# Weight preparation moved into the attention layer; power weights and message products as split halves on Trainium2

## The reference, cut to what matters

```python
# layer 0: masked attention
A = exp(tanh(x @ q @ (x @ k).T / sqrt(D) / 8) * 8) * adj; A = A / A.sum(-1)
x = layernorm(x + A @ x @ v)
# layer 1: gated, 5 steps, m_in = m_out = adj @ h
u3 = h @ u3_w.T + u3_b
z = sigmoid(av @ w3_w.T + w3_b + u3);  r = sigmoid(av @ w4_w.T + w4_b + u3)
hv = tanh(av @ w5_w.T + w5_b + (r * h @ u5_w.T + u5_b));  h = (1 - z) * h + z * hv
# layer 2: powers 0 to 3 of the adjacency, each with weights of its own
y = sum_k adj^k @ x @ weight_k        # both adjacencies are adj: weights 1..3 are summed in pairs
x = layernorm(x + y)
# layer 3: messages
f = relu(x @ psi_w + psi_b); m = (adj * adj).T @ f
h = relu(concat(m, x) @ phi1_w + phi1_b); x = layernorm(x + h @ phi2_w + phi2_b)
```

## Time and profile before

| | |
|---|---|
| median of 3 runs | 1480.62 us (1480.22, 1480.62, 2062.51) |
| profiled execution | 1478.63 us, span 1476.8 us |
| TensorE busy | 1405.0 us (95%) |
| TensorE weight load busy | 1223.4 us (83%) |
| VectorE busy | 1048.6 us (71%) |
| ScalarE busy | 930.1 us (63%) |
| GpSimd busy | 671.1 us (45%) |
| mean granted TensorE clock | 0.981 |

### The profile page before, as it was taken

The page is one execution under the profiler, slowest core; times in us unless marked ns, Lnnn a source line. Parts: engine busy times, 40 slices in busy tenths (PEclk is TensorE's granted clock), DMA queues, the critical chain, the costliest instruction groups (busy, mean ns, idle before and its releaser), DMA issues. The chain is left out here.

```text
span 1476.8 us, 27170 instructions
## 1 busy us (share of the span) xinstructions
PE 1405.0 (95%) x8813; PEld 1223.4 (83%) x8813; DVE 1048.6 (71%) x2558; ACT 930.1 (63%) x1666; POOL 671.1 (45%) x628
## 2 busy tenths in 40 slices
PE   3999996999999999999999999997699999999995
PEld 3888885888888888888888888886699999999993
DVE  2788884777777777777777777776466666666663
ACT  1666663677776777767777677775356566556653
POOL 0111113666687666786666866667222222211122
PEclk9999997999999999999999999999799999999998
DMA  2111111000000000010000100000001111111101
GB/s 75 37 43 43 43 35 57 1 0 0 0 34 25 1 0 0 19 38 0 0 0 4 53 0 0 0 0 14 30 22 44 44 43 43 43 43 43 36 25 32
DMA packets 46063, 35.76 MB, mean 24 GB/s; under 512 B 3140, under 2 KB 37704, under 8 KB 46024
## 3 DMA queue, kind: packets, MB, share of 16 engines
q1 hardware_dynamic: 46024, 35.27, 7.4%
HBM read 10.10 MB, written 8.39 MB: 13 GB/s over the span
## 5 line engine op out<-in xcount | busy, mean ns | idle before, releaser
L540 POOL TENSOR_TENSOR rh_lo<-rh,rh_hi 128x512 fp32r<-128x512 f32 x160 | 207.0, 1294 | 229.4 <-ACT rh_hi L661 219.7
L820 POOL TENSOR_TENSOR c_rstd<-c_var_eps,c_minus_half 128x12 f32<-128x12 f32 x37 | 84.0, 2270 | 347.3 <-DVE c_var_eps L1048 347.3
L546 POOL TENSOR_TENSOR h_lo<-h,h_hi 128x512 fp32r<-128x512 f32 x160 | 208.1, 1301 | 12.8
L675 DVE TENSOR_TENSOR psum<-psum,h 128x512 f32<-128x512 f32 x160 | 111.9, 700 | 105.1 <-ACT psum L665 105.1
L661 ACT CAST rh_hi<-rh 128x512 fp32r<-128x512 f32 x160 | 99.9, 624 | 121.2 <-DVE rh L693 121.2
L594 PE MATMUL psum<-adj_t_hi,hn_hi 128*128 128x256 f32 x640 | 172.6, 303 | 0.6 <-DVE m_lo L687 0.6
L658 ACT ACTIVATE psum<-psum,bias_cols 128x512 f32<-128x512 f32 x160 | 106.0, 662 | 105.8 <-PE psum L612 105.8
L693 DVE TENSOR_TENSOR rh<-psum,h 128x512 f32<-128x512 f32 x160 | 110.7, 692 | 70.8 <-ACT psum L658 70.7
L596 PE MATMUL psum<-adj_t_hi,hn_lo 128*128 128x256 f32 x640 | 159.4, 283 | 0.0
L832 PE MATMUL psum<-wcat,x2t 128*128 128x128 f32 x1024 | 137.2, 277 | 0.7 <-ACT x2t L984 0.7
L832 PEld LDWEIGHTS psum<-wcat,x2t 128*128 128x128 f32 x1024 | 126.5, 194 | 1.6 <-ACT x2t L984 1.1
(11 more groups left out here) (161 smaller groups left out, 3875.3 us busy)
## 6 DMA issues: line engine op xcount, KB each, us to landing
x_in<-in_x_dram SPq DMA_DIRECT2D x32, 256.0 KB, 2.8
h<-state SPq DMA_DIRECT2D x32, 256.0 KB, 2.3
y1t<-state SPq DMA_DIRECT2D x32, 256.0 KB, 2.4
out_dram<-res SPq DMA_DIRECT2D x32, 256.0 KB, 2.3
conv_in<-in_L_gnn_weight_dram SPq DMA_DIRECT2D x1, 448.0 KB, 3.3
w_in<-in_L_gnn_w_w_dram SPq DMA_DIRECT2D x3, 128.0 KB, 2.3
adj_n<-in_adj_dram SPq DMA_DIRECT2D x1, 256.0 KB, 2.7
u_in<-in_L_gnn_u_w_dram SPq DMA_DIRECT2D x2, 64.0 KB, 2.3
```

Of the source, the lines that this page charges most:

```text
L540: pool.tensor_tensor(rh_lo[:, q, :], rh[:, q, :], rh_hi[:, q, :].bitcast(F32), ALU.subtract).then_inc(rh_lo_done, 1)
L546: pool.tensor_tensor(h_lo[:, q, :], h[:, (g - 1) % G, :], h_hi[:, q, :].bitcast(F32), ALU.subtract).then_inc(h_lo_done, 1)
L675: dve.tensor_tensor(cb, cb, hg, ALU.subtract).then_inc(dif_done, 1)
```

## The change

`setup` as a stage goes; its work stands in `attention_layer`. SyncE issues the first input tile first, then the adjacency, then between the input tiles the gate weights (slot 1) and the rest (slot 3). ScalarE's queue issues q, k and v. TensorE transposes q, k and the adjacency ahead of slot 0 and the gate weights after slot 1. GpSimd sums the gate weights and the power weights, and splits the power weights `wcat` (in reversed order of powers) into `wc_hi`, `wc_lo` and `phi1m` into `phi1m_hi`, `phi1m_lo`. The gate weights lie in joint tiles (`wg_hi`, `ug_hi`), with the same products in the gated layer.

In `graph_conv_layers` x2 transposed is split (`x2t_hi` by ScalarE, `x2t_lo` by VectorE), and `weights(q, pair, c)` makes three fp32r products of 256 columns for each batch: two powers at once. PSUM banks 0 and 1 hold powers 3 and 2, banks 2 and 3 powers 1 and 0, each power in one half of both banks (`power(j)`). The message is split too (`msg_hi`, `msg_lo`), and `phi1m` is three fp32r products in place of one fp32 product, behind `phi1x`, which waits for the message no more. The bias of `phi2` is added to x3 by GpSimd (`x3b`) in place of the product L919.

The diff, cut to its core (left out are declarations, the removed `setup`, the renamed gate weights, and the other hi and lo copies that follow `power(j)`):

```diff
+        def run(eng, slot, lags, weights=None):
 
             for it in range(PEELED):
                 for u in range(U):
                     slot(it, u)
+                    if weights is not None and (it, u) == (0, 1):
+                        weights()
...
+                if isinstance(it, int) and s == 0:
+                    sp.dma_start(adj_n[:, :, :], t["adj"].rearrange("(c p) m -> p c m", p=128)).then_inc(adj_loaded, 16)
+                if isinstance(it, int) and s == 1:
+                    for i, name in enumerate(("L1_gnn_w3_w", "L1_gnn_w4_w", "L1_gnn_w5_w")):
+                        sp.dma_start(w_in[:, i, :], t[name]).then_inc(w_loaded, 16)
+                    for i, name in enumerate(("L1_gnn_u3_w", "L1_gnn_u5_w")):
+                        sp.dma_start(u_in[:, i, :], t[name]).then_inc(w_loaded, 16)
+                    for i, name in enumerate(("L1_gnn_w4_b", "L1_gnn_w3_b", "L1_gnn_w5_b", "L1_gnn_u3_b", "L1_gnn_u5_b")):
+                        sp.dma_start(bias_cols[:, i:i + 1], t[name].rearrange("(p o) -> p o", o=1)).then_inc(w_loaded, 16)
+                if isinstance(it, int) and s == 3:
+                    sp.dma_start(conv_in[:, :], t["L2_gnn_weight_1"].rearrange("i o k -> i (o k)")).then_inc(conv_loaded, 16)
...
+                    sp.dma_start(phi1m[:, :], t["L3_gnn_phi1_w"][0:D, :]).then_inc(phi1m_loaded, 16)
+                    sp.dma_start(env["phi2_b"][:, :], t["L3_gnn_phi2_b"].rearrange("(o d) -> o d", o=1).broadcast_to([128, D]))\
+                      .then_inc(rest_loaded, 16)
...
+            pool.wait_ge(w_loaded, 16 * 10)
+            for i, src in enumerate((1, 2, 0)):
+                op = pool.tensor_tensor(w_sum[:, i, :], w_in[:, src, 0:D], w_in[:, src, D:2 * D], ALU.add)
+            op.then_inc(w_summed, 1)
+            pool.wait_ge(w_summed, 1)
+            pool.tensor_tensor(w_dif[:, :], w_sum[:, 2, :], w_sum[:, 0, :], ALU.subtract).then_inc(w_ready, 1)
...
+            pool.tensor_copy(wcat[:, 3, :], by_power[:, 0, :])
+            for j in range(1, 4):
+                op = pool.tensor_tensor(wcat[:, 3 - j, :], by_power[:, j, :], by_power[:, j + 3, :], ALU.add)
+            op.then_inc(wcat_done, 1)
+            pool.wait_ge(wcat_done, 1)
+            pool.tensor_copy(wc_hi[:, :, :], wcat[:, :, :]).then_inc(wc_hi_done, 1)
+            pool.wait_ge(phi1m_loaded, 16)
+            pool.tensor_copy(phi1m_hi[:, :], phi1m[:, :]).then_inc(wc_hi_done, 1)
...
+            pool.tensor_tensor(wc_lo[:, :, :], wcat[:, :, :], wc_hi[:, :, :].bitcast(F32), ALU.subtract)
+            pool.tensor_tensor(phi1m_lo[:, :], phi1m[:, :], phi1m_hi[:, :].bitcast(F32), ALU.subtract)
...
+                    if isinstance(it, int) and s == 0:
+                        pe.wait_ge(qk_done, 1)
                     pe.matmul(psum[:, B_P, :], qk[:, :], x_t[:, u % 2, :], start=True, stop=True).then_inc(p_mm, 1)
...
+                    if isinstance(it, int) and s == 0:
+                        pe.wait_ge(v_loaded, 16)
...
+            def weights():
+
+                pe.wait_ge(w_ready, 1)
+                for i in range(2):
+                    pe.transpose(psum[:, B_U, i * D:(i + 1) * D], u_in[:, i, :], ident[:, :])
+                for i, w in enumerate((w_sum[:, 0, :], w_sum[:, 1, :], w_dif[:, :])):
+                    mm = pe.transpose(psum[:, B_W, i * D:(i + 1) * D], w, ident[:, :])
+                mm.then_inc(w_turned, 1)
+
+            pe.wait_ge(ident_done, 1)
+            pe.wait_ge(qk_loaded, 32)
+            pe.transpose(psum[:, B_QKT, 0:D], q_in[:, :], ident[:, :])
+            pe.transpose(psum[:, B_QKT, D:2 * D], k_in[:, :], ident[:, :]).then_inc(qk_turned, 1)
+            pe.wait_ge(adj_loaded, 16)
+            for k in range(KC):
+                for c in range(KC):
+                    mm = pe.transpose(psum[:, B_ADJ, k * N + c * 128:k * N + c * 128 + 128],
+                                      adj_n[:, c, k * 128:(k + 1) * 128], ident[:, :])
+            mm.then_inc(adj_turned, 1)
+            pe.wait_ge(qk_t_done, 1)
+            pe.matmul(psum[:, B_QK, 0:D], qk_t[:, 0, :], qk_t[:, 1, :], start=True, stop=True).then_inc(qk_mm, 1)
+            run(pe, slot, LAG_TURN, weights)
...
+            act.dma_start(q_in[:, :], t["L0_gnn_q"]).then_inc(qk_loaded, 16)
+            act.dma_start(k_in[:, :], t["L0_gnn_k"]).then_inc(qk_loaded, 16)
+            act.dma_start(v[:, :], t["L0_gnn_v"]).then_inc(v_loaded, 16)
...
+            dve.wait_ge(qk_turned, 1)
+            dve.tensor_copy(qk_t[:, :, :], psum[:, B_QKT, 0:2 * D].rearrange("p (k n) -> p k n", k=2)).then_inc(qk_t_done, 1)
+            dve.wait_ge(qk_mm, 1)
+            dve.tensor_copy(qk[:, :], psum[:, B_QK, 0:D]).then_inc(qk_done, 1)
+            dve.wait_ge(adj_turned, 1)
+            dve.tensor_copy(adj_t[:, :, :], psum[:, B_ADJ, :].rearrange("p (k n) -> p k n", k=KC)).then_inc(adj_t_done, 1)
+            dve.tensor_copy(adj_t_hi[:, :, :], psum[:, B_ADJ, :].rearrange("p (k n) -> p k n", k=KC))
+            dve.wait_ge(w_turned, 1)
...
+        def power(j):
+
+            pair, half = (3 - j) // 2, (3 - j) % 2
+            return psum[:, B_C + 2 * pair:B_C + 2 * pair + 2, half * 256:half * 256 + 256]
+
...
+                if live(it, u, L_F):
+                    n = s - L_F
+                    pool.wait_ge(x3_done, n + 1)
+                    wait_count(pool, y3_done, n - 1)
+                    pool.tensor_tensor(x3b[:, (u - L_F) % 2, :, :], x3[:, (u - L_F) % 4, :, :],
+                                       phi2_b[:, :].rearrange("p (o d) -> p o d", o=1).broadcast_to([128, TILES, D]),
+                                       ALU.add).then_inc(x3b_done, 1)
...
-            def weights(n, q, j):
-
-                for b in range(GB):
-                    for c in range(KC):
-                        i = tile(b, c)
-                        mm = pe.matmul(psum[:, B_C + j, cols(i)], x2t[:, q, cols(i)], wcat[:, j, :],
-                                       start=(b == 0 and c == 0), stop=(j == 3), skip_group_check=True)
-                mm.then_inc(w_mm[j], 1)
+            def weights(q, pair, c):
+
+                for which, w in ((x2t_hi, wc_hi), (x2t_hi, wc_lo), (x2t_lo, wc_hi)):
+                    for b in range(GB):
+                        dst = psum[:, B_C + 2 * pair + c, :].rearrange("p (j b d) -> p j b d", j=2, b=GB)[:, :, b, :]
+                        mm = pe.matmul(dst, which[:, q, cols(tile(b, c))], w[:, 2 * pair:2 * pair + 2, :],
+                                       start=(b == 0 and which is x2t_hi and w is wc_hi), stop=(which is x2t_lo),
+                                       skip_group_check=True)
+                return mm
 
             def spread(n, level):
...
-                    dst = psum[:, B_C + 2 - level, c * GB * D:(c + 1) * GB * D]
+                    dst = power(2 - level)[:, c, :]
                     for k in range(KC):
...
-                    wait_count(pe, c_lo_done[0], w)
-                    weights(w, wq, 3)
+                    pe.wait_ge(x2t_lo_done, w + 1)
+                    wait_count(pe, c_lo_done[1], w)
+                    for c in range(KC):
+                        mm = weights(wq, 0, c)
+                    mm.then_inc(w_mm[0], 1)
...
                     mm.then_inc(y1_mm, 1)
                 if live(it, u, L_W):
 
-                    wait_count(pe, c_lo_done[1], w)
-                    weights(w, wq, 2)
+                    wait_count(pe, y2_done, w)
+                    weights(wq, 1, 0)
                     spread(w, 0)
                 if live(it, u, L_F):
...
                     mm.then_inc(msg_mm, 1)
                 if live(it, u, L_W):
 
-                    wait_count(pe, c_lo_done[2], w)
-                    weights(w, wq, 1)
+                    weights(wq, 1, 1).then_inc(w_mm[1], 1)
                     spread(w, 1)
                 if live(it, u, L_F):
 
-                    pe.wait_ge(msg_done, m + 1)
                     pe.matmul(psum[:, B_F, :], phi1x[:, :], x3t[:, :], start=True, stop=False)
-                    pe.matmul(psum[:, B_F, :], phi1m[:, :], msg[:, :], start=False, stop=True).then_inc(hid_mm, 1)
+                    pe.wait_ge(msg_hi_done, m + 1)
+                    pe.matmul(psum[:, B_F, :], phi1m_hi[:, :], msg_hi[:, :], start=False, stop=False)
+                    pe.matmul(psum[:, B_F, :], phi1m_lo[:, :], msg_hi[:, :], start=False, stop=False)
+                    pe.wait_ge(msg_lo_done, m + 1)
+                    pe.matmul(psum[:, B_F, :], phi1m_hi[:, :], msg_lo[:, :], start=False, stop=True).then_inc(hid_mm, 1)
                 if live(it, u, L_T2):
...
-                    wait_count(pe, y2_done, w)
-                    weights(w, wq, 0)
                     spread(w, 2)
                 if live(it, u, L_F):
 
                     pe.wait_ge(hid_done, m + 1)
-                    pe.matmul(psum[:, B_M, :], ones[:, :], flat(phi2_row[:, :, :]), start=True, stop=False,
-                              skip_group_check=True)
```

(19 more changed lines are left out.)

287 lines of the change are left out of this document (114 added, 173 removed).

## The result

The changed kernel takes 1458.3 us (median of 4 runs, 1456.0 to 1459.0) against 1480.4 before. The ratio is 0.9855, 95% interval 0.9834 to 0.9876: about 22 us, clear of noise but inside the 2% band. One run of before (2062.5 us) and one of experiment 3 (1515.5 us) are slow and stand outside the ratios. The predicted time was 1452 us. The profiled execution took 1458.58 us, 1456.7 of it the span, 20.1 less than the 1476.8 of before.

What follows compares the result with a forecast made beforehand. TensorE's own work was taken to bound the last layers. Start 18.0, slots 6.5, ramp 0.3 and tail 3 summed to 27.8 us off the median 1480.62, giving 1452 us; own range 1446 to 1459, 8 in 10 range 1438 to 1460.

Steps and rivals of the forecast that it cites:

- The forecast case: Whole kernel: early first input, a new TensorE wait per last-layer slot, 1452 us; chance 0.73.
- The start: Attention layer's beginning: without the setup stage, work on the first input tile starts earlier, gaining 18.0 us (16.5 to 19.5).
- TensorE's work of a slot: Last layers: split products cut TensorE's work per slot from 12.65 to 11.5 us, 33 us were it the only bound.
- no new wait: Rival for the last layers: x2t_lo or msg_lo holds nothing up, slots of 11.5 to 11.7, 1427 us; chance 0.12.
- The circle: Last-layer slots: chain through msg_lo, statistics, pow, x3, x2t_lo and x3 transposes makes a slot 12.44 us, leaving 6.5 us gain.
- 12 products (pair 0) 1.41: Last-layer slot's opening on TensorE: its first 12 split weight products end 1.41 us after the first one's start.
- The ramp: Slots 2 and 3, waiting on chains that the change shortens by a few 0.1 us: 0.3 us gained.
- waits on chains that the change shortens: Slots 2 and 3: the chains they wait on become a few 0.1 us shorter, 0.3 us gained.
- The tail: Last two slots: phi1x no longer waits for msg, gaining 3 us (1 to 4).
- The start gives less: Rival for the kernel's beginning: loads land late or GpSimd's list outlasts its cover, 1456 to 1462 us; chance 0.12.
- Slower by the clock: Rival for the last-layer slots: standing still 1 us lowers TensorE's clock, up to 11.5 us more per slot; chance 0.02.
- Slower by the write pattern: Rival for the weight products: writing two PSUM runs of 128 columns slows them, 1655 us at the fp32 rate; chance 0.01.

Runs made afterwards that it cites:

- experiment 3: Changed kernel with an extra 128x512 VectorE addition once a slot, right behind msg_lo and ahead of the combined statistics; 1478.8 us, ratio 1.0001 against before.
- experiment 4: Only the attention layer and weight preparation of the changed kernel, with the layers of the kernel before behind them; 1459.4 us, ratio 0.9878 against before.
- experiment 7: Changed kernel with both moves: msg_lo behind the combined statistics and x2t_lo ahead of x3; 1427.4 us, ratio 0.9658 against before.
- experiment 8: Start of the changed kernel with the layers of before, plus only the message split, msg_lo in the change's place; 1454.8 us, ratio 0.9858 against before.
- experiment 1: Changed kernel with msg_lo moved on VectorE from in front of the combined statistics to behind them; 1427.0 us, ratio 0.9655 against before.
- experiment 6: Changed kernel with x2's transposes ahead of the last power weights, x2t_hi ahead of hid, x2t_lo ahead of x3; 1440.0 us, ratio 0.9746 against before.
- experiment 2: Changed kernel with an extra 128x512 VectorE addition once a slot, behind the third c_lo; 1460.2 us, ratio 0.9888 against before.
- experiment 9: Changed kernel with the psi_row product once more per slot, output unused, ahead of the x3 transposes; 1458.5 us, ratio 0.9869 against before.

## Why the prediction was right, and where its sizes were off

The forecast case held: the start gives its share, a new wait takes the place of TensorE's work, and the slots gain little. The number held less well: 1458.3 us lies near the upper end of the forecast's own range (1446 to 1459) and of the wide one (1438 to 1460). The start came as forecast, and the other three terms all gave less than I had put on them. Term by term, in us of the span:

**The start, 18.0 predicted, 18.4 measured** (the layer's first transposes, 1032.60 before, 1014.16 after; experiment 4 gives 19.2 over its whole span). The agreement to 0.4 is closer than one trace against one can tell: with the first transposes at 1011.7 to 1014.3, as in the traces named above, the start would be worth 18.3 to 20.9. Slot 0's transposes came at 6.61 where I had 6.3. The five transposes of the gate weights took 0.54 us, below my 0.6 to 1.1. GpSimd's preparation ended at 20.8, and I had 21.

**TensorE's work of a slot, 11.5 predicted, 11.51 to 11.59 measured.** In the changed kernel it is the slot of 12.54 less the 1.03 us of standing still. In experiment 7, with no wait left and the transposes of x2 in a new place, it is 11.59. The message's part, 0.16, was 0.18 in experiment 8. The rival of "no new wait" had put its time for this case at 1427 us; experiments 1 and 7, which take the wait away, took 1427.0 and 1427.4 (ratios 0.9655 and 0.9658, where 1427 of 1480.6 is 0.964).

**The circle, a slot of 12.44 predicted, 12.576 measured; 6.5 us predicted, 2.5 measured.** The links and their order were right: L946 waits for x2t_lo, x3 for the power, the power for the statistics behind msg_lo, and experiments 1, 3 and 6 move the time through three of them. This is the term whose size was off, by 0.14 us a slot, and three steps make it up. "12 products (pair 0) 1.41" was 1.50, from 1225.04 to 1226.54: the first pair, behind the transposes, takes 0.32, the others 0.24, so the power came 7.99 us into the slot and not 7.91. The x3 transposes began 12.16 us in and not 11.97; I had them 0.04 us behind x2t_lo's end, and they come 0.15 behind it (they themselves took 0.38 and not 0.47, which gives 0.09 back). And most slots are 12.55, but the one at each turn of the loop is 12.77 (five of the 29), which I had left out of the 12.44, though the 12.665 of before contains such slots. I had written that 0.15 us a slot are 4.4 us; it was 0.14 and 4.0.

**The ramp, 0.3 gained predicted, 1.1 lost.** From the layer's first transposes to the first psi_row it is 36.23 us where it was 35.05, and TensorE stands still for 12.8 of them where it stood still for 11.3. Here the step "waits on chains that the change shortens" failed. The waits of TensorE in the ramp of the changed kernel:

```profile
1036.88 0.39 PE L858 MATMUL psum<-c_hi,adj_t_hi 128*128 128x256 f32 x1 [0.96 <-DVE c_lo L1019]
...
1043.54 0.38 PE L858 MATMUL psum<-c_hi,adj_t_hi 128*128 128x256 f32 x1 [0.68 <-DVE c_lo L1019]
1046.15 0.38 PE L858 MATMUL psum<-c_hi,adj_t_hi 128*128 128x256 f32 x1 [0.96 <-DVE c_lo L1019]
1048.49 0.63 PE L946 MATMUL psum<-ident,x 128*128 128x128 f32 x4 [1.13 <-DVE x2t_lo L1083]
```

In these slots, which are not full, TensorE waits for c_hi and c_lo whatever its own work is, and x2t_lo is one link more. With the powers alone the ramp is 36.23 too, with the messages alone 34.81 (1013.03 to 1047.84), and with x2t_lo ahead of x3 35.57. So the loss is the powers' part, and 0.66 of it hangs on where x2t_lo stands, as long as the clock holds (in experiment 7 it did not, and the ramp is 37.22).

**The tail, 3 predicted, 0.3 measured.** Half of what I had worked out came: phi1x no longer waits for msg, and the last two slots took 21.91 us (1415.10 to 1437.01), 1.45 less than the 23.36 of before (1434.88 to 1458.24). What I had put at nothing is a wait for x3 and the clock behind it, TensorE's timeline:

```profile
1435.68 0.65 PE L946 MATMUL psum<-ident,x 128*128 128x128 f32 x4 [1.83 <-DVE x L1076]
1437.01 0.79 PE L879 MATMUL psum<-psi_row,ones 128*128 128x512 f32 x1 [0.68 <-ACT x3t L964]
1437.60 1.91 PE L882 MATMUL psum<-psi,x3t 128*128 128x128 f32 x8
```

The transposes of x3 wait 1.83 us, for a power that stands behind msg_lo; before, they follow phi2 after 0.89 us (1456.08 to 1456.97), and in experiment 1, with msg_lo moved, after 0.99. Then psi_row takes 0.79 us and psi 1.91, where in experiment 4 the same rows took 0.50 and 1.05. From there to the end it is 19.7 us, 1.1 more than the 18.6 of before; in experiments 1 and 7 it is 18.9. The windows view of the 2.4 us from the last psi_row on gives the reason, the changed kernel first and experiment 1 second:

```profile
1437.01:1439.41 2.40, 2.40 (x9) 2.11 (x9) 0.12 (x1) 0.00 (x0) 0.00 (x0) 0.50 0.00 0
1409.41:1411.81 2.40, 1.39 (x9) 1.15 (x9) 0.86 (x4) 0.97 (x3) 0.00 (x0) 1.00 0.00 0
```

The granted clock is 0.50 there, the lower of the two levels, and the same nine matmul instructions keep TensorE busy for all of the 2.40 us and not for 1.39. In all twelve traces it goes with the wait: where TensorE had stood still 1.57 to 2.21 us before the last transposes of x3 (the changed kernel, experiments 2, 3, 6 and 9) the granted clock of these 2.4 us is 0.50 to 0.70 and the stretch takes 19.7 to 21.6 us; in the seven traces without that wait it is 1.00 and 18.4 to 18.9. No experiment changed this wait and nothing else, so that the wait brings the clock down is likely and not shown.

Sum: 18.4 + 2.5 - 1.1 + 0.3 = 20.1 us, where I had 27.8.

**The rivals.** "No new wait" is refuted for this kernel by the 0.87 us row. "The start gives less" did not happen. "Slower by the clock": the granted clock is 1.00 over the slots, with 1.03 us of standing still in each; against before only the last stretch has less of it. "Slower by the write pattern": the products that write two runs of 128 columns follow each other at 0.24 us a pair, 0.12 each, and those that write one run of 256 (L858, L860) at 0.114 to 0.1175. The Trainium skill ("PSUM — Partial Sum Buffer", Specifications) says that any non-contiguous pattern slows matmuls significantly; for runs of 128 fp32 values the trace does not agree. The other place that I cited, the Trainium skill ("TensorE: Matmul & The Clock Gate", Back-to-back issue gap), has 109 ns for 256 columns, and the power products of after stay at 117 to 120, so keeping the row was the better choice; by an estimate with the 109 ns of the Trainium skill the circle would have come out shorter still, and further off.
